# Last slot of both graph layers in three node blocks, its keys and values stored first in two parts, and the last edge pair of layer two in 8 and 4 tiles

## The reference

```python
edge_index = jnp.stack([src, dst])          # sorted by dst
# layer 1: 4 heads of 32
xl = (x @ W_lin.T).reshape(N, 4, 32)
alpha = (xl[dst]*att_src).sum(-1) + (xl[src]*att_dst).sum(-1) + (ef*att_edge).sum(-1)
alpha = softmax over the edges of a target (leaky_relu(alpha, 0.2))
out = segment_sum(xl[src] * alpha[..., None], dst) + bias + x
x1 = layernorm(x + elu(layernorm(out) * gamma + beta))
# layer 2: 8 heads of 16
q, k, v = x1 @ Wq.T, x1 @ Wk.T, x1 @ Wv.T
alpha = sum(q[dst] * edge_attr_128 * k[src], -1) / sqrt(16) * edge_weight
return layernorm(x1 + segment_sum(alpha[..., None] * v[src], dst))
```

## Time and profile before

| | |
|---|---|
| median of 3 runs | 4164.89 us |
| profiled execution | 4166.46 us |
| its span, first to last instruction | 4164.8 us |
| granted TensorE clock, mean | 0.592 |
| busy: PE / VectorE / ACT / GpSimd | 1931.6 / 2554.3 / 256.5 / 3064.1 us |
| layer 1 | 0 to about 2117 us |
| layer 2 | about 2117 to 4165 us |

### The profile page before, as it was taken

How to read it: one execution, slowest core, us unless ns; L and a number is a source line. 1 busy time by engine, 2 the same in 40 slices (tenths; PEclk the granted TensorE clock), 3 DMA queues, 4 the chain that set the end, 5 groups by cost and what they waited for, 6 DMA issues and landing times.

```text
span 4164.8 us, 43395 instructions
## 1 busy us (share of the span) xinstructions
PE 1931.6 (46%) x10576; PEld 1624.9 (39%) x10576; DVE 2554.3 (61%) x4276; ACT 256.5 (6%) x646; POOL 3064.1 (74%) x3247
## 2 busy tenths in 40 slices
PE   4644445545444555544524444444444444444444
PEld 2433234333232333333424444444444444444444
DVE  3555555655555566555656666666666666676666
ACT  1101101100111110001100000000000000000000
POOL 7777777777777777777357777777777777777775
PEclk6666666776666676766755555555555555555555
DMA  8444445444444544444256666666666666666664
GB/s 207 132 135 118 120 125 140 128 140 125 121 119 121 139 131 137 125 127 119 77 193 222 211 222 216 215 223 213 223 212 212 223 215 222 214 219 219 210 222 134
DMA packets 357908, 711.10 MB, mean 171 GB/s; under 512 B 126483, under 2 KB 214548, under 8 KB 344676
## 3 DMA queue, kind: packets, MB, share of 16 engines
q0 software_dynamic: 129504, 324.46, 28.4%
q1 hardware_dynamic: 181880, 354.74, 25.5%
q10 hardware_dynamic: 46476, 31.39, 2.4%
HBM read 682.18 MB, written 28.15 MB: 171 GB/s over the span
## 4 chain that ended last, share of the span: by engine, by line
POOL 40%; issue 19%; DVE 14%; DVEq 13%; PE 9%; DMA 4%; ACT 1%; POOLq 0%; SPq 0%; ACTq 0%
POOL ring L1323 27%; POOL ring L576 13%; DVEq L913 5%; DVE work L916 5%; PE psum L1352 4%; DMA ring<-kv_table,den_cols 2%; PE psum L698 2%; DVE ring L1516 1%; DVEq L1503 1%; DVEq L1498 1%; DVEq L1507 1%; DVEq L73 1%; DMA dst_pair<-dst_row_dram 1%; DVE work L1013 1%; DVE work L1016 0%
## 5 line engine op out<-in xcount | busy, mean ns | idle before, releaser
L576 POOL DMA_INDIRECT ring<-x_table,idx x1584 | 1499.5, 947 | 483.0 <-issue 459.9
L1323 POOL DMA_INDIRECT ring<-kv_table,den_cols x1516 | 1433.3, 945 | 461.8 <-issue 452.0
L1352 PE MATMUL psum<-work,ring 128*128 128x42 f32 x3232 | 712.4, 420 | 425.1 <-DVE ring L1516 425.1
L1352 PEld LDWEIGHTS psum<-work,ring 128*128 128x128 f32 x3232 | 697.0, 332 | 454.0 <-DVE ring L1516 454.0
L1494 DVE TENSOR_TENSOR psum<-psum,ring 128x2048 f32<-128x2048 f32 x101 | 232.3, 2300 | 584.5 <-DMA ring<-kv_table,den_cols 550.9
L698 PE MATMUL psum<-work 128*42 128x132 f32 x3232 | 491.1, 316 | 189.5 <-DVE work L1016 189.5
L1345 PE MATMUL psum<-ring,work 126*128 126x128 bf16 x1616 | 190.7, 312 | 702.3 <-DVE ring L1500 678.3
L698 PEld LDWEIGHTS psum<-work 128*42 128x42 f32 x3232 | 412.9, 137 | 246.4 <-DVE work L1016 220.4
L1345 PEld LDWEIGHTS psum<-ring,work 126*128 126x128 bf16 x1616 | 164.1, 146 | 718.1 <-DVE ring L1500 693.4
L916 DVE TENSOR_TENSOR work<-dst_pair,psum 126x1024 bf16<-126x1024 int32 x204 | 249.2, 1221 | 74.9 <-issue 43.0
L1016 DVE TENSOR_TENSOR work<-ring,psum 128x1056 f32 (+1 forms) x202 | 251.3, 1244 | 0.0
(11 more groups left out here) (202 smaller groups left out, 2076.7 us busy)
## 6 DMA issues: line engine op xcount, KB each, us to landing
dst_pair<-dst_row_dram SPq DMA_DIRECT2D x204, 512.0 KB
dst_pair<-dst_row_dram SPq DMA_DIRECT2D x101, 1024.0 KB
ring<-ea_dram SPq DMA_DIRECT2D x101, 1024.0 KB, 5.5
ring<-x_table,idx POOLq DMA_INDIRECT x1584
ring<-kv_table,den_cols POOLq DMA_INDIRECT x1516, 2.8
ea_pair<-ea_turned_dram SPq DMA_DIRECT2D x102, 128.0 KB
kv_table<-work ACTq DMA_DIRECT2D x17, 512.0 KB, 3.1
q_table<-work ACTq DMA_DIRECT2D x17, 384.0 KB, 3.9
```

Source lines behind the costliest of these rows:

```text
L576: pool.indirect_dma_start(x_rows[:, h * CHUNK_TILES + t, :], None, k["x_table"], bass.IndirectOffsetOnAxis(idx[h][:, t:t + 1], 0))\
L1323: pool.indirect_dma_start(kv[p % BUFS][:, t, :], None, k["kv_table"], bass.IndirectOffsetOnAxis(index[:, tile:tile + 1], 0))\
L1352: last = pe.matmul(sum_ps[u], message[e][:, u * GROUP + t, :], onehot[e][:, u * GROUP + t, :], start=t == 0, stop=t == GROUP - 1)
```

## The change

The last slot of both layers is worked in three blocks of 128 nodes (`FIN_LAST`) in place of four. The count of passes now also takes the last slot's span in steps of 384: (span + 383) times 43, shifted right by 14. The slot's end stays `NODE_ROWS`. In the last visit of layer 1 the keys and values are made, copied and stored ahead of the queries, in two stores (256 nodes, then 128) with a semaphore each. In layer 2 the last pair is worked as 8 tiles and then 4, each from its own gather semaphore, the last sums go to three PSUM places, and the last visit's inverse root is one GpSimd instruction in place of 13 of VectorE.

```diff
+FIN_LAST = 3
+LAST_MUL, LAST_SHIFT = 43, 14
...
-def rows_start(eng, reg, fin_row, slot, pass_no):
+def rows_start(eng, reg, fin_row, slot, pass_no, nb):
...
-    eng.reg_add(reg, reg, pass_no * FIN_NODES)
-    eng.reg_alu(reg, reg, NODE_ROWS - FIN_NODES, op=ALU.min)
+    eng.reg_add(reg, reg, pass_no * (nb * P))
+    eng.reg_alu(reg, reg, NODE_ROWS - nb * P, op=ALU.min)
...
         dve.tensor_reduce(out=fin_passes, in_=fin_span, axis=AX.X, op=ALU.max)
+        dve.tensor_scalar(last_passes, fin_span[:, CHUNKS - 1:CHUNKS], FIN_LAST * P - 1, None, ALU.add)
         dve.drain()
         dve.tensor_scalar(fin_passes, fin_passes, FIN_NODES - 1, None, ALU.add)
+        dve.tensor_scalar(last_passes, last_passes, LAST_MUL, None, ALU.mult)
         dve.drain()
         dve.tensor_scalar(fin_passes, fin_passes, 9, None, ALU.arith_shift_right)
+        dve.tensor_scalar(last_passes, last_passes, LAST_SHIFT, None, ALU.arith_shift_right)
+        dve.drain()
+        dve.tensor_tensor(out=fin_passes, in0=fin_passes, in1=last_passes, op=ALU.max)
         dve.drain()
         dve.tensor_tensor(out=passes_sb, in0=passes_sb, in1=fin_passes, op=ALU.max).then_inc(prologue_over, 1)
...
+            if last_slot:
+                for half, half_out in enumerate((kv_out, kv_last_out)):
+                    copy_key_values(v, half, nb)
+                    act.drain()
+                    n = min(2, nb - 2 * half)
+                    act.dma_start(k["kv_table"][bass.DynSlice(start + half * 2 * P, n * P), :]
+                                  .rearrange("(b p) f -> p b f", p=P),
...
+                       .then_inc(half_out, 16)
+                copy_query(v, nb)
...
+            with pool.Fori(0, passes) as again:
+                wait_here(pool, var_made, pool.snap(last_visit) + 1, pool_gate)
+                root = rstd[:, 0:FIN_LAST]
+                pool.tensor_tensor(out=root, in0=root, in1=k["half_neg"][:, 0:FIN_LAST], op=ALU.pow).then_inc(pool_root_made, 1)
...
+        def last_sums(n, e, r):
+            wait_here(pe, rows_made, pe.snap(fin_visit) + 1, pe_gate)
+            pe.wait_ge(last_made, r + 1)
+            for u in range(2):
+                if u:
+                    pe.wait_ge(msg_made, n + MSG_CREDIT + 1)
+                to = last_sum_ps if u == 0 else sum_ps[1]
+                for t in range(LAST_TILES_OF[u]):
+                    last = pe.matmul(to, message[e][:, u * GROUP + t, :], onehot[e][:, u * GROUP + t, :],
+                                     start=t == 0, stop=t == LAST_TILES_OF[u] - 1)
+                last.then_inc(last_summed if u == 0 else summed, 1)
...
+        def last_pair(e, buf, group, uses, turn, r, sums_of):
+            for u in range(2):
+                n = LAST_TILES_OF[u]
...
+                dve.wait_ge(last_kv_in[u], 16 * n * (r + 1))
...
```

More of the change, by code:

```diff
@@ L721, in turn_slot, with key_values @@
             wait_here(pe, x1T_copied, v + 1, pe_gate)
-        def key_values(half):
-            for u in range(2):
+        def key_values(half, nb):
+            for u in range(min(2, nb - 2 * half)):
                 b = 2 * half + u
@@ L842, in finish_slot @@
             act.wait_ge(x1_turned, v + 1)
[L843 to L851, removed]
+            act.activation(x1T[:, 0:nodes], y_ps[:, 0:nodes], ACT.Copy).then_inc(x1T_copied, 1)
@@ new lines, in finish_slot @@
+            if last_slot:
+                for half, half_out in enumerate((kv_out, kv_last_out)):
[4 more added lines that the diff above has]
+                                  .rearrange("(b p) f -> p b f", p=P),
+                                  kv_rows[:, half * FIN_NODES:half * FIN_NODES + n * 2 * FEAT].rearrange("p (b f) -> p b f", b=n))\
+                       .then_inc(half_out, 16)
+                copy_query(v, nb)
+            else:
+                copy_query(v, nb)
+                for half in range(2):
+                    copy_key_values(v, half, nb)
+                act.drain()
+                act.dma_start(rows_of(k["kv_table"]), kv_rows.rearrange("p (b f) -> p b f", b=FIN)).then_inc(kv_out, 16)
@@ L852, in finish_slot @@
             act.wait_ge(q_split, v + 1)
[L853 to L855 removed]
+            act.dma_start(k["q_table"][bass.DynSlice(start, nodes), :, :].rearrange("(b p) s f -> p b (s f)", p=P),
+                          q_rows[:, 0:nb].rearrange("p b s f -> p b (s f)")).then_inc(fin_out, 16)
@@ L1373, in chunk @@
                     finish()
-                sums(n + i, i % 2)
+                if last_chunk and i + 1 == pairs:
+                    last_sums(n + i, i % 2, r)
+                else:
+                    sums(n + i, i % 2)
             pe.reg_add(done, done, pairs)
@@ L1413, in finish @@
                 act.drain()
-                act.dma_start(rows_of(k["out"]), blocks(o)).then_inc(written, 16)
+                act.dma_start(rows_of(k["out"]), blocks(o, nb)).then_inc(written, 16)
                 act.reg_add(fin_visit, fin_visit, 1)
@@ L1466, in finish @@
+        def finish(last_slot=False):
+            nb = FIN_LAST if last_slot else FIN
+            nodes = nb * P
             with dve.Fori(0, passes) as r:
                 v = dve.snap(fin_visit)
+                v_last = dve.snap(last_visit)
                 wait_here(dve, x1_in, 16 * (v + 1), dve_gate)
                 wait_here(dve, fin_turned, v + 2, dve_gate)
-                dve.tensor_tensor(out=y_ps, in0=y_ps, in1=x1_fin, op=ALU.add).then_inc(x1_used, 1)
+                dve.tensor_tensor(out=y_ps[:, 0:nodes], in0=y_ps[:, 0:nodes], in1=x1_fin[:, 0:nodes], op=ALU.add)\
+                   .then_inc(x1_used, 1)
@@ L1496, in chunk @@
                     dve.wait_ge(summed, turn)
-                    add(0, sums_of[0])
+                    add(sum_ps[0], sums_of[0])
                 dve.drain()
```

223 lines of the change are left out of this document (145 added, 78 removed).

## The result

| | before | after |
|---|---|---|
| median | 4164.27 us (4 runs) | 7516.96 us |
| ratio after / before, 95% interval | | 1.8044 [1.802, 1.8068] |
| profiled execution / its span | 4166.46 / 4164.8 us | 7517.19 / 7515.4 us |
| mean granted TensorE clock | 0.592 | 0.602 |

One of the four executions after took 7816.25 us; it was disturbed and is left out.

What follows compares the result with a forecast made beforehand. Both layers were taken to go at the gather's pace, with bare ends; a span of 442 rows makes two passes. Terms summing to +3387 us on the 4164.8 us span gave 7552 us, range 7430 to 7690.

Steps and rivals of the forecast that it cites:

- rival A: Pass count stays 1 and only the two ends move, -8.9 and -12.2 us: 4144 us; chance 3%.
- Items 1 and 2: Start of the kernel: preparation instructions +0.3 us, scores of the first chunk done once more +36 us.
- Item 3: Layer 1, chunks 0 to 15: second pass 54.8 and second visit 38.4, so 195.8 us a chunk; +1225 us.
- Rival C: Two passes, layer 1's second visit hides its stores, gap 5 instead of 12.2 us: 7437 us; chance 6%.
- rival D: Two passes, PE's clock at half through the groups, each of 34 passes up to 15 us longer: about 8060; 4%.
- The rule beside the row: x1's 256 KB store: 2.6 us by the skill's rule against the row's 4.3; sum 7523 us by the rule.
- Items 4 and 5: Layer 1's last groups once more, +26.5 us; last slot's two visits to layer 2's first gather, +22 (10 to 32).
- Item 8: Doubled slot visits inside layer 2: GpSimd waits about 1.2 us at each of 32 for PE's sums; +38 (0 to 130).
- Rival B: Two passes, layer 2's doubled visits not hidden, 12.5 us lost each time, 400 instead of 38: 7914 us; 6%.
- Item 6: Layer 2 between passes: second pass's gathers start 26.9 us behind the first's last, then take 2014.9; together +2041.8 us.
- Item 7: End of the kernel: 30.2 us behind the last gather instead of 32.4; -2.2 us.

Runs made afterwards that it cites:

- the first experiment: Changed kernel with the last slot's end at 6250 instead of 6400, so one pass; rows from 6341 set by two small stores: 4148.98 us against 4167.31, ratio 0.9955.
- the one-pass kernels: Follow-up kernels whose loops run one pass, with all or part of the change; measured from 4147.87 to 4158.17 us.
- root put back: One-pass version of the changed kernel, with the last layer 2 visit's inverse root made by VectorE again: 4147.87 us against 4165.42, ratio 0.9956.
- seam only: One pass; the changed kernel's layer 1 with layer 2 of the kernel before: 4158.17 us against 4166.78, ratio 0.9982.
- tail only: One pass; layer 1 of the kernel before with the changed kernel's layer 2: 4157.79 us against 4166.78, ratio 0.9977.
- four blocks: Changed kernel with the last slot in four blocks (FIN_LAST = 4), slot's end still 6400, one pass: 4155.29 us against 4166.78, ratio 0.9973.

## Why the prediction was right, step by step

The mechanism was right: two passes by the arithmetic of the last slot's span, which was 443 (442 forecast; rival A needs 379 or less, and the first experiment made it by hand). 7552 was forecast and 7517 came, 35 less. Four terms were mis-sized; the rest stood within a microsecond.

- **Items 1 and 2**: the first chunk's L980 at 168.7 us, forecast 168.5.
- **Item 3, chunks**: 194.6 us, forecast 195.8. The second pass took 54.3 (54.8), the second visit 37.5 (38.4). Its gap was 11.8 (12.2): the store came 2.3 us behind VectorE, as forecast, ACT began 5.1 and not 5.8 behind its issue, and L1084 4.3 and not 4.1 behind that. VectorE's own part was 25.7, not 26.2. Times 16: -19 us. Rival C (gap 5) and rival D (half clock; it was 0.93 and 0.87 in the two passes) did not come.
- **The rule beside the row**: x1's store landed 4.0 us after its issue (median), with two others in flight. By the rule of the Trainium skill (DMA: Bandwidth & Descriptors, Anatomy of one DMA) my estimate was 2.6; the trace agrees with it where it is the only store in flight, the output of the same 256 KB at 2.7, and not where three are. The section's figures are for transfers that GpSimd issues; both of these are ACT's. That the sum by the rule, 7523, lies nearer to 7517 than mine is luck: it would have ACT begin 4.1 us behind the store's issue, where it took 5.1, and most of the miss is elsewhere.
- **Items 4 and 5**: from the last L980 to the first gather of layer 2 it took 125.1 us, forecast 126.1. VectorE was the last to release that gather, 2.2 us behind its visit, as forecast; the smaller store landed in 1.7 to 2.1 us, where I had 3 to 4, which changed nothing. Inside the seam, by the one-pass kernels, three blocks were worth 4.6 to 5.9 us at one visit, all told; I had taken 3.6 for the shortened instructions alone.
- **Item 8, stops behind slot visits**: I took 1.2 us for each of 32, +38. The passes took 2019.6 and 2020.0 us against the bare 2014.9: +9.8. The waits for PE's sums at tile 12 are there, but only seven in the two passes are longer than the usual 0.3 us, between 1.1 and 1.5. One of them, and the sum over the layer (below L1368 in the single lines; before has 9.7 us in 32):

```profile
5146.99 0.94 POOL L1368 DMA_INDIRECT ring<-kv_table,den_cols  x1 [1.38 <-PE psum L1403]
```

```profile
  PE psum L1403: 26.2, 62
```

  The term had the right place and a third of a microsecond for a size: I had the stop of 1.2 us in all 32 slots, and seven have it, because the margin varies from slot to slot and I had read it in one. Rival B, the whole visit lost each time, did not come. At pair 96, the place of the earlier trace rows, the trace shows the order that I forecast:

```profile
7420.45 0.69 DVE L1577 TENSOR_TENSOR psum<-psum,ring 128x512 f32<-128x512 f32 x1
...
7431.45 6.89 PE L1403 MATMUL psum<-work,ring 128*128 128x42 f32 x32
7432.74 0.70 DVE L1577 TENSOR_TENSOR psum<-psum,ring 128x512 f32<-128x512 f32 x1 [6.97 <-DMA ring<-x_table]
...
7438.27 2.30 DVE L1607 TENSOR_TENSOR psum<-psum,ring 128x2048 f32<-128x2048 f32 x1 [0.20 <-issue]
...
7467.34 2.29 DVE L1607 TENSOR_TENSOR psum<-psum,ring 128x2048 f32<-128x2048 f32 x1
...
7472.48 0.20 DVE L1530 TENSOR_TENSOR sumT<-sumT,psum 128x42 f32 x1 [2.85 <-PE psum L1403]
```

  PE's sums end at 7438.34, and the gather that needs them (31 before the last, at 7479.09 - 38.8 = 7440.3) finds them 1.9 us early, where I had it 1.0 us late: the first L1577 stands 58.6 us ahead of the last gather, and L1470 stood 56.4 ahead in before.

- **Item 6, the hole**: 33.0 us, forecast 26.9. VectorE begins the last pair of the first pass 4.7 us later than forecast (3.45 us behind the start of the last gather, where I had 1.2 ahead), so the last add stands 15.7 behind the last gather's end and not 10.9. I had written that VectorE catches up within two pairs. It does so nearly: in the second pass pair 99 starts at 7467.34, 11.8 us ahead of the last gather, against 12.2 where each slot is visited once (7462.25 against 7474.48). But the next add then waits 2.85 us for PE's sums of pair 98, which were started late, and with one visit it doesn't wait. VectorE had caught up, and PE's sums, one pair behind it, had not; I had left them out. The step from GpSimd's root to its first gather was 2.9, where I had 1.2.
- **Item 7, the end**: 35.4 us, forecast 30.2. The same lateness gives 3.6. Another 2.2 are the longer end behind the last store: GpSimd's closing drain ends 6.3 us behind its root, and I had priced the root as if nothing followed it. The root put back (end 2.3) shows that part.
- **The sum of the misses**: chunks -19, item 8 -28, hole +6, end +5, seam -1: -37 on the span, of 7552.

## What to carry to other kernels

When an edit changes a number that a loop's trip count is made from, work that count out on the real data, padding included, before pricing anything else: here 6400 in place of 6250 as the slot's end, together with blocks of 384 in place of 512, turned two edits worth 18 us into a loss of 3350. Where an engine gets a small job at the end of its queue, look at what stands behind it in the next pass; but time won by an early start is only won if the engines that feed the next wait are free too. At the very end of a kernel, look at what stands behind the job as well: GpSimd's root saved 1.5 us on the chain, and GpSimd's closing drain behind it cost 2.5. And a kernel that seems bound by one engine can have a second pace-setting wait under it, which shows only when the first is taken away, as the pause at tile 72 did.

## What the runs showed of the hardware that I had not expected

- GpSimd's closing drain ended 6.3 us behind GpSimd's last piece of work, whether that was a gather (before, the kernel before with two passes, seam only, root put back: 6.3 in each) or the root (whole change with one pass, tail only, four blocks, after: 6.3 in each). With the root the span therefore ended 4.8, 4.8, 4.5 and 4.8 us behind the issue of the last store; without it 2.6, 2.5 and 2.3 (before, seam only, root put back).
- The same gather took 956 ns in the first pass of layer 2 and 945 in the second, within one execution. On a path of 3,224 gathers 6 ns on the mean are 19 us, more than both edits are worth.
- TensorE was granted 0.93 in the first and 0.87 in the second of two passes with the same instructions. It was busy 38.9 and 42.0 us of the 54, and both passes took the same time.
- The store of keys and values landed in 3.1 us in the median and in 7.2 at the seam of before, where the first gather waited for it. In two parts of 256 and 128 KB no part took longer than 2.1.
